# Four-layer image stack on one core: attention sums, one order in the Fourier stage, and all loops written out

## The chip, the cores and the metric

One Trainium2 chip, one of its cores. The metric is the device time of one execution in microseconds; the median of three runs of the kernel before is 20360.88 us (20354.01 to 20361.54).

## The reference, cut to what matters

The input `x` is 2 images of 64 channels, 256 x 256, fp32, held as 128 channels by L = 65536 pixels. Four layers follow one another, each on the group-normalized result of the one before and added to it:

```python
x = x + _L0_conv_ref(_gn(x), img, w_pos, w_img, w_comp)   # attention over 9 shifted neighbours
x = x + _L1_conv_ref(_gn(x), ...)                         # two state-space scans ("mamba") along the pixels
x = x + _L2_conv_ref(_gn(x), w_in, w_dw, fft_filter, w_out) # 8x8 Fourier patches, 3x3 taps, gelu gate
x = x + _L3_conv_ref(_gn(x), q_table, 1)                  # 8x8 cosine transform, rounded

# layer 0
un_em = _unfold3x3(em)                                    # em: 64 maps from image and position
feature_score = jnp.einsum('bckhw,bchw->bkhw', un_em, em)
un_fea = _unfold3x3(inp)
comp_score = jax.nn.sigmoid(jnp.einsum('bckhw,c->bkhw', un_fea, w_comp))
weighted_fea = jnp.einsum('bckhw,bkhw->bchw', un_fea, comp_score * feature_score)
# layer 1, per state n of 16, twice
h = dA_t * h + dBu_t;  y = einsum(h, C_t)
# layer 2
x = einsum(x, w_in); xf = rfft2(patches) * fft_filter; x = irfft2(xf)
x = depthwise 3x3 conv(x); x1, x2 = split(x); x = gelu(x1) * x2; einsum(x, w_out)
```

## The kernel before

Six stages run one after another, each a block in which the five engines have their own instruction streams and meet at semaphores: statistics of x, score maps, attention, mamba, Fourier, cosine transform. Every stream issues in order, so an instruction that waits holds up all that is behind it on its engine.

**Attention** (`attention_layer`, L385 to L680): 64 chunks of 1024 pixels, and a 65th step for the rest. A step has nine neighbours k. TensorE (PE) spreads the score map of k over the channels in PSUM (`p_f`, two banks taken in turns); VectorE (DVE) multiplies it by the shifted input `g` into `apr` k (L657, in the code `pr[k]`); GpSimd (Pool) adds products in pairs (L678): (0,1), (2,3), (4,5), (6,7), and 8 onto 6. PE sums the four results with identity matmuls into `p_a` (`add`, L519 through the helper `halves`): 0, 2, 4 at k = 6, 7, 8 of the step, the last one, 6, at k = 2 of the next. DVE then writes the output (`output`, L632, at k = 4), its statistics (L645, k = 6) and the next `g` (`make_g`, L623, at k = 7). `g` is the input less its mean, times a sigmoid; ScalarE (ACT) reads the score `p_s` from PSUM and writes the sigmoid to SBUF as `sig` (L582), so `make_g` reads two SBUF tiles, `ax` and `sig`.

**Mamba** (`mamba_layer`, L683 to L1377): 64 chunks of 1024, each in four tasks (two layers l, two images b), a task for 16 states n. For 13 of them DVE multiplies (L1305) and then scans (L1311); for three (8, 9, 10) Pool makes the product and DVE only scans. Each scan waits for DVE's own product of the same state (L1307). Pool multiplies every state by C (L1359), PE adds over states (`py`, L1016), ACT makes the decays (L1176). A "turn" is four tasks; turns 2 to 62 of the chunks lie in a loop (L829), 61 times; a turn before it and one behind it, and two tasks at either end, are written out. At the loop's head ACT loads an activation table (L1186). Once in a turn DVE takes the statistics of the output (L1283) and once in a task it gates (L1278).

**Fourier** (`fft_layer`, L1380 to L1992): 64 slots, two for each of 32 stripes of 8 rows. A slot is 24 ticks on PE: `conv` (L1620, taps of unit u), `project` (L1628, L1630: the output product of the slot before, in two parts at ticks 1 and 4), `widen` (L1594: pair p of the next slot, at ticks 1, 3, ... 15), `from_freq` (L1603), and in even slots `turn` and `to_freq` for the next stripe. DVE multiplies what `widen` left in the single PSUM tile `p_fr` by the filter (`filter_`, L1854); it has 30 taps per slot (L1848), the filter of pair p stands ahead of tap 3, 5, 8, ..., and the residual additions (L1870) behind taps 3 and 7.

**Loops.** In every stage a part of the turns is a hardware loop with a counter in a register (L37, L44, L458, L829, L1551, L1684, L1796, L1905, L1974, L2031, L2053); there the semaphore values of waits are computed by register instructions ahead of the wait. Outside of the loops they are constants.

## Time and profile before

| | |
|---|---|
| median of three runs | 20360.88 us |
| the profiled execution | 20351.94 us |
| its span | 20350.2 us |
| attention | about 390 to 1560 us |
| mamba | about 1650 to 16410 us |
| Fourier | about 16523 to 19890 us |
| cosine transform | about 19975 us to the end |
| busy, share of the span: PE, DVE, ACT, Pool | 67%, 90%, 56%, 85% |

The shares are averages over stages that have different limits, so each stage is read for itself. Instructions of registers, branches and semaphores are not counted as busy.

### The profile page before, as it was taken

What the parts mean: (1) busy time and instruction counts of PE and PEld (TensorE: products, weight loads), DVE (VectorE), ACT (ScalarE), POOL (GpSimd) and SP (SyncE); (2) the same over time, 40 slices, a digit from 0 to 9 for tenths busy, and PEclk for the clock granted to TensorE, in tenths of its full rate; (3) what the DMA queues carried; (4) which work ended last, traced back from release to release, by engine and by line L of the source; (5) the groups of instructions that cost most, each with busy time, mean ns of one, the idle gap of its engine ahead of it and who ended that gap; (6) DMA issues with size and microseconds to landing.
All of it is one profiled execution on the core that took longest, in us unless ns stands there. A gap on an engine that the chain in (4) does not pass through costs nothing. (4 is left out here: it accounts for less than half of the span.)

```text
span 20350.2 us, 184019 instructions
## 1 busy us (share of the span) xinstructions
PE 13599.4 (67%) x47074; PEld 4943.0 (24%) x47074; DVE 18393.4 (90%) x11898; ACT 11461.6 (56%) x12716; POOL 17198.0 (85%) x7352
## 2 busy tenths in 40 slices
PE   4885666666666666666666666666666668888885
PEld 2331111111111111111111111111111134444444
DVE  5778999999999999999999999999999978888896
ACT  1115666666666666666566666666666646666663
POOL 3777888888888988888888888888888968888881
PEclk8887777777777777777777777777777789999997
DMA  3224555555545555555555455554555511011113
GB/s 120 94 91 121 134 127 126 129 130 134 128 126 128 131 133 129 126 128 132 131 131 127 127 131 131 131 127 127 130 132 130 128 41 31 25 31 31 31 27 137
DMA packets 615483, 2240.63 MB, mean 110 GB/s; under 512 B 74881, under 2 KB 92147, under 8 KB 591091
## 3 DMA queue, kind: packets, MB, share of 16 engines
q1 hardware_dynamic: 610146, 2232.63, 42.2%
q10 hardware_dynamic: 5265, 7.14, 0.1%
q8 instruction: 33, 0.54, 0.0%
q14 instruction: 39, 0.32, 0.0%
HBM read 990.77 MB, written 174.96 MB: 57 GB/s over the span
## 5 line engine op out<-in xcount | busy, mean ns | idle before, releaser
L1359 POOL TENSOR_TENSOR h<-h,c_bc 128x1024 f32<-128x1024 f32 x4096 | 9620.9, 2359 | 1534.0 <-DVE h L1311 1494.3
L1311 DVE TENSOR_TENSOR_SCAN h<-da,state,px 128x1024 f32<-128x1024 f32 x3328 | 7810.9, 2347 | 559.2 <-PE py L1016 168.6
L1176 ACT ACTIVATE da<-d_bc,a_neg 128x1024 f32<-128x1024 f32 x3328 | 3796.6, 1145 | 3500.2 <-DVE h L1311 3476.0
L1002 PE MATMUL px<-cf,bsel 32*128 32x512 f32 x4096 | 2023.6, 1083 | 3854.4 <-DVE h L1311 3854.4
L1305 DVE TENSOR_TENSOR px<-px,du_bc 128x1024 f32<-128x1024 f32 x3328 | 4099.1, 1232 | 287.8 <-PE px L1002 70.5
L1948 POOL TENSOR_TENSOR acc<-acc,ta 128x1024 f32<-128x1024 f32 (+1 forms) x1040 | 2424.8, 2339 | 492.5 <-DVE acc L1848 366.9
L1016 PE MATMUL py<-h,ysel 128*32 128x512 f32 x16384 | 2393.2, 710 | 96.8 <-POOL h L1359 96.1
L1848 DVE SCALAR_TENSOR_TENSOR p_c<-zb,w_dw,p_c 128x1024 f32<-128x1024 f32 (+1 forms) x1560 | 1987.0, 1274 | 43.7 <-PE p_c L1620 11.2
L1351 POOL TENSOR_TENSOR xs<-du_bc,b_bc 128x1024 f32<-128x1024 f32 x768 | 1807.7, 2354 | 0.0
L1311 DVE TENSOR_TENSOR_SCAN h<-px,state,xs 128x1024 f32<-128x1024 f32 x768 | 1743.1, 2326 | 0.0
L1002 PEld LDWEIGHTS px<-cf,bsel 32*128 32x128 f32 x4096 | 488.7, 290 | 4993.7 <-DVE h L1311 4635.0
L1747 ACT ACTIVATE ta<-zb,w_dw 128x1024 f32<-128x1024 f32 (+1 forms) x1040 | 1168.7, 1128 | 308.7 <-POOL acc L1948 286.9
L1603 PE MATMUL p_i<-basis,v 128*128 128x128 f32 x6144 | 964.4, 294 | 382.9 <-ACT zb L1726 372.8
L1176 ACT ACTIVATE px<-d_bc,a_neg 128x1024 f32<-128x1024 f32 x768 | 855.2, 1114 | 634.1 <-DVE h L1311 630.4
L973 PE MATMUL pm<-hx,w_tap 128*128 128x512 f32 x1024 | 794.0, 946 | 532.8 <-ACT hx L1084 532.8
L678 POOL TENSOR_TENSOR apr<-apr 128x1024 f32<-128x1024 f32 x325 | 824.1, 2543 | 383.4 <-DVE apr L657 377.9
L1620 PE MATMUL p_c<-zb,diag 128*128 128x512 f32 x2064 | 1016.8, 627 | 167.2 <-DVE acc L1848 132.5
L1603 PEld LDWEIGHTS p_i<-basis,v 128*128 128x128 f32 x6144 | 779.6, 193 | 811.1 <-ACT zb L1726 553.7
L1016 PEld LDWEIGHTS py<-h,ysel 128*32 128x32 f32 x16384 | 472.8, 121 | 1891.0 <-issue 1227.0
L657 DVE TENSOR_TENSOR apr<-g,p_f 128x1024 f32<-128x1024 f32 x585 | 690.0, 1214 | 253.5 <-PE p_f L519 252.1
L981 PE MATMUL pm<-hy,w_res 64*128 64x512 f32 x512 | 482.8, 1096 | 620.1 <-ACT u L1094 620.1
L1726 ACT ACTIVATE zb<-p_i 128x384 f32<-128x384 f32 x1024 | 524.4, 512 | 645.9 <-PE p_i L1603 641.7
(222 smaller groups left out, 20126.8 us busy)
## 6 DMA issues: line engine op xcount, KB each, us to landing
d_bc<-delta SPq DMA_DIRECT2D x1024, 512.0 KB, 8.3
du_bc<-du SPq DMA_DIRECT2D x1024, 512.0 KB, 8.2
c_bc<-c_rows_dram SPq DMA_DIRECT2D x1024, 512.0 KB, 4.5
b_bc<-c_rows_dram SPq DMA_DIRECT2D x256, 512.0 KB, 7.9
hx<-x_dram SPq DMA_DIRECT2D x252, 256.5 KB, 5.3
st_x<-in_x_dram SPq DMA_DIRECT2D x32, 1024.0 KB, 4.8
ax<-in_x_dram SPq DMA_DIRECT2D x64, 512.0 KB, 3.4
xr<-x_dram SPq DMA_DIRECT2D x64, 512.0 KB, 5.8
```

What stands on the lines that cost most here:

```text
L1002: last = nc.tensor.matmul(px[(t.par + q + q // 2) % 2][:, cut], bsel[rows, q, :], cf[rows, cut], start=True, stop=True)
L1016: last = nc.tensor.matmul(py[32 * j:32 * j + 32, cut], ysel[:, :], h[:, (4 * q + j) % 8, cut], start=False, stop=(q == Q - 1))
L1176: nc.scalar.activation(out[:, :], d_bc[:, n % J, :], ACT.Exp, scale=a_neg[t.l][:, n:n + 1]).then_inc(da_done, 1)
L1305: nc.vector.tensor_tensor(out=x[:, :], in0=b[:, :], in1=du_bc[:, j, :], op=ALU.mult).then_inc(m1_done, 1)
L1311: nc.vector.tensor_tensor_scan(h[:, n % 8, PAD:T + PAD], a[:, :], x[:, :], state[:, 2 * t.l + t.b, n:n + 1], ALU.mult, ALU.add).then_inc(s ...
L1351: nc.gpsimd.tensor_tensor(out=xs[i][:, :], in0=du_bc[:, n % J, :], in1=b_bc[:, :], op=ALU.mult).then_inc(xs_done, 1)
L1359: nc.gpsimd.tensor_tensor(out=h[:, n % 8, 0:T], in0=h[:, n % 8, PAD:T + PAD], in1=c_bc[q % 2][:, :], op=ALU.mult).then_inc(m2_done, 1)
L1603: last = nc.tensor.matmul(p_i[:, c], v[j // 2 % 2][:, j % 2, c], basis[:, 1, :], start=True, stop=True)
L1620: last = nc.tensor.matmul(p_c[odd(s, u)][:, i * 512:i * 512 + rows * W], diag[:, oc, t, :], zb[b][:, oc, y:y + rows, dx:dx + W], start=(t ...
L1747: nc.scalar.activation(ta[odd(s, u)][t][:, 0:n * W].rearrange("p (y x) -> p y x", y=n), zb[b][:, oc, y:y + n, dx:dx + W], ACT.Identity, sc ...
L1848: nc.vector.scalar_tensor_tensor(out=out, in0=zb[b][:, oc, y:y + n, dx:dx + W], scalar=w_dw[:, oc, m:m + 1], in1=other, op0=ALU.mult, op1= ...
L1948: nc.gpsimd.tensor_tensor(out=acc[h][oc][:, c], in0=acc[h][oc][:, c], in1=ta[o][t][:, c], op=ALU.add).then_inc(added, 1)
```

## The change

Attention: Pool gets a sixth addition, (0,2), after (2,3), and PE adds three results (0 at k = 7, 4 at k = 8, 6 at k = 2 of the next step) instead of four. The sigmoid is written over the score in PSUM; `make_g` reads it there, and the next score waits until `make_g` has read (`g_done`) instead of for the sigmoid. Fourier: in a slot on PE `widen` stands ahead of `project`. All loops are written out: every step, turn and slot is in the program with constant addresses and semaphore values; the table load at the head of the mamba loop is left out.

```diff
-        sig = [sb(f"sig{i}", [128, T]) for i in range(2)]
...
-        PAIRS = [(0, 1), (2, 3), (4, 5), (6, 7), (6, 8)]
-        SUMMED = {0: 1, 2: 2, 4: 3, 6: 5}
+        PAIRS = [(0, 1), (2, 3), (0, 2), (4, 5), (6, 7), (6, 8)]
+        SUMMED = {0: 3, 4: 4, 6: 6}
+        NP, NA = len(PAIRS), len(SUMMED)
...
-                for c in range(3):
-                    step(Step(0, c))
-                with eng.Fori(1, NK // 2 - 1) as m:
-                    for c in (1, 2):
-                        step(Step(m, c))
-                for c in (NK - 1, NK):
-                    step(Step(0, c))
+                for c in range(NK + 1):
+                    step(Step(c))
...
                 if s.from_(1):
-                    pe.wait_ge(sig_done, s.nth(0, 1) - 1)
+                    pe.wait_ge(g_done, s.nth(0, 1) - 1)
                 halves(p_s, comp_s[:, :], x[s.par]).then_inc(s_ps, 1)
...
-                    if k >= 6:
-                        add(s, 2 * (k - 6))
+                    if k == 7:
+                        add(s, 0)
+                    if k == 8:
+                        add(s, 4)
...
-                    if s.from_(2):
-                        act.wait_ge(g_done, s.nth(0, 1) - 2)
-                    nc.scalar.activation(sig[s.par][:, :], p_s[:, :], ACT.Sigmoid, bias=s_bias[:, :]).then_inc(sig_done, 1)
+                    nc.scalar.activation(p_s[:, :], p_s[:, :], ACT.Sigmoid, bias=s_bias[:, :]).then_inc(sig_done, 1)
...
-                                               in1=sig[s.par][:, :], op0=ALU.add, op1=ALU.mult).then_inc(g_done, 1)
+                                               in1=p_s[:, :], op0=ALU.add, op1=ALU.mult).then_inc(g_done, 1)
...
-                    if s.from_(1) and k % 2 == 0 and k < 8:
-                        dve.wait_ge(acc_done, s.nth(k // 2, 4) - 4)
+                    if s.from_(1) and k in SUMMED:
+                        dve.wait_ge(acc_done, s.nth(list(SUMMED).index(k), NA) - NA)
...
-                    if n == 4:
-                        pool.wait_ge(paired, s.nth(3, 5))
+                    if n in (2, NP - 1):
+                        pool.wait_ge(paired, s.nth(n - 1, NP))
...
-            with eng.Fori(2, NK - 1) as k:
-                tasks = turn_tasks(k, k, -2)
...
+        for k in range(1, NK):
+            TASKS += turn_tasks(k)
...
-                if not isinstance(t.turn, int) and t.c == -2:
-                    act.preload_act_table_set("natural_log_exp_and_others")
...
                     if j in CONV_AT:
                         conv(s, b, CONV_AT[j])
+                    if not no_next and j in WIDEN_AT:
+                        widen(ns, r + b, nb, WIDEN_AT[j])
                     if not first and j in PROJECT_AT:
                         project(s - 1, nb, r if rows_left else None, PROJECT_AT.index(j))
                     if not no_next:
-                        if j in WIDEN_AT:
-                            widen(ns, r + b, nb, WIDEN_AT[j])
...
-            with pe.Fori(1, NR - 1) as r:
+            for r in range(1, NR - 1):
```

The other loops (statistics, cosine transform, the other engines of the Fourier stage) are changed like the last one.

## Rows read from the trace of the kernel before

**Rows 1.** Busy time in stretches: us, PE, PEld, DVE, ACT, POOL, PEclk, DMA share, GB/s

```profile
390.00:1560.00 1170.00, 965.66 (x2464) 372.83 (x2462) 906.27 (x846) 139.29 (x128) 824.12 (x325) 0.89 0.28 91
1650.00:16410.00 14760.00, 9397.27 (x28604) 2722.43 (x28604) 13937.42 (x7791) 8945.76 (x9622) 13232.59 (x5683) 0.73 0.51 129
16523.00:19890.00 3367.00, 2752.20 (x13593) 1468.15 (x13591) 3011.12 (x2677) 2118.23 (x2628) 2997.59 (x1274) 0.97 0.11 29
```

**Rows 2.** One line's instructions: the mamba loop's branch on DVE, durations in ns, first and last start

```profile
L829 DVEq COMPARE_BRANCH  x61: 50/56/67, 2187.9 to 16046.1; - x61
```

**Rows 3.** Timeline of DVE: its gates, in written-out tasks before and behind the mamba loop

```profile
1744.60 1.20 DVE L1278 TENSOR_TENSOR yg<-py,sr 128x1024 f32<-128x1024 f32 x1
...
1970.78 1.20 DVE L1278 TENSOR_TENSOR yg<-py,sr 128x1024 f32<-128x1024 f32 x1
...
16059.42 1.20 DVE L1278 TENSOR_TENSOR yg<-py,sr 128x1024 f32<-128x1024 f32 x1
...
16287.41 1.20 DVE L1278 TENSOR_TENSOR yg<-py,sr 128x1024 f32<-128x1024 f32 x1
```

**Rows 4.** Groups by line: statistics in mamba, and the table load; busy us, mean ns

```profile
L1283 DVE BATCH_NORM_STATS2 bn_even<-xo 128x512 f32 (+1 forms) x128 | 80.7, 673 | 16.9 <-POOL xo L1342 16.9
L1186 ACT ACT_TABLE_LOAD x61 | 78.3, 1283 | 1.1
```

**Rows 5.** Waits of DVE, 1963 to 16048 us (mamba loop): us in total, times, longest

```profile
DVE h L1311 <- DVE px L1305: 111.4, 488, 0.3
```

**Rows 6.** Timeline of DVE at a back edge of the mamba loop

```profile
6809.81 1.23 DVE L1305 TENSOR_TENSOR px<-px,du_bc 128x1024 f32<-128x1024 f32 x1
6811.32 2.35 DVE L1311 TENSOR_TENSOR_SCAN h<-da,state,px 128x1024 f32<-128x1024 f32 x1 [0.28 <-DVE px L1305]
```

**Rows 7.** DMA queues in a written-out stretch, 1650 to 1957 us: packets, MB, share

```profile
q8 instruction: 5, 0.08, 0.1%
q14 instruction: 6, 0.05, 0.0%
```

**Rows 8.** DMA queues within the mamba loop, 2187 to 16046 us: the only one listed

```profile
q1 hardware_dynamic: 497314, 1793.55, 51.1%
```

**Rows 9.** Pool's additions in attention: durations min/median/max in ns, first and last start

```profile
L678 POOL TENSOR_TENSOR apr<-apr x325: 2334/2356/3345, 396.2 to 1551.5; 128x1024 f32<-128x1024 f32 x163
```

**Rows 10.** Timeline of Pool over one attention step: start us, us, idle before

```profile
1025.47 2.36 POOL L678 TENSOR_TENSOR apr<-apr 128x1024 f32<-128x1024 f32 x1 [3.12 <-DVE apr L657]
...
1032.37 8.07 POOL L678 TENSOR_TENSOR apr<-apr 128x1024 f32<-128x1024 f32 x3 [1.09 <-DVE apr L657]
1041.95 2.35 POOL L678 TENSOR_TENSOR apr<-apr 128x1024 f32<-128x1024 f32 x1 [1.51 <-DVE apr L657]
```

**Rows 11.** Timeline of DVE over the same step

```profile
1026.44 1.28 DVE L632 SCALAR_TENSOR_TENSOR axo<-p_a,a_gn,axr 128x1024 f32<-128x1024 f32 x1
...
1032.21 1.28 DVE L623 SCALAR_TENSOR_TENSOR g<-ax,mean_n,sig 128x1024 f32<-128x1024 f32 x1
...
1040.65 2.35 DVE L657 TENSOR_TENSOR apr<-g,p_f 128x1024 f32<-128x1024 f32 x2 [2.38 <-PE p_f L519]
```

**Rows 12.** Waits of DVE, 16786 to 19741 us (Fourier)

```profile
DVE v L1854 <- PE p_fr L1594: 278.6, 224, 3.9
```

**Rows 13.** Timeline in an even Fourier slot that began at 16834.9 us

```profile
16838.71 1.98 PE L1628 MATMUL p_qo<-ge,w_out 128*64 128x512 f32 x4
...
16841.67 0.92 PE L1594 MATMUL p_fr<-w_in,ft 64*128 64x384 f32 x4
16842.73 0.96 DVE L1854 TENSOR_TENSOR v<-p_fr,filt 128x768 f32<-128x768 f32 x1 [3.93 <-PE p_fr L1594]
...
16843.74 0.92 PE L1594 MATMUL p_fr<-w_in,ft 64*128 64x384 f32 x4 [1.16 <-DVE v L1854]
```

**Rows 14.** Timeline in the odd slot behind it

```profile
16896.69 0.96 DVE L1854 TENSOR_TENSOR v<-p_fr,filt 128x768 f32<-128x768 f32 x1 [1.27 <-PE p_fr L1594]
...
16897.70 0.92 PE L1594 MATMUL p_fr<-w_in,ft 64*128 64x384 f32 x4 [1.16 <-DVE v L1854]
```

More of the change, by code:

```diff
@@ L36, in _ @@
                 eng.dma_start(xt[i][:, :], src[:, i * T:(i + 1) * T]).then_inc(x_in[i], 16)
-            with eng.Fori(1, NK // 2) as k:
+            for k in range(1, NK // 2):
                 for i in range(2):
@@ L43, in _ @@
         def _(eng):
-            with eng.Fori(0, NK // 2) as k:
+            for k in range(0, NK // 2):
                 for i in range(2):
@@ L549, in step @@
                         score(s.other(1))
[L550 to L553 removed]
+                    if k == 7:
+                        add(s, 0)
+                    if k == 8:
+                        add(s, 4)
+            score(Step(0))
             run(step)(pe)
[L555 removed]
+            add(Step(NK), 6)
         @block.scalar
@@ L664, in step @@
                         make_g(s.other(1))
-            make_g(Step(0, 0))
+            make_g(Step(0))
             run(step)(dve)
-            output(Step(0, NK))
-            statistics(Step(0, NK))
+            output(Step(NK))
+            statistics(Step(NK))
         @block.gpsimd
@@ L877, in spread_b @@
             def spread_b(t):
-                stored = eng.to_reg(16 * t.nth()) if not isinstance(t.turn, int) else 16 * t.nth()
                 if t.from_(1):
                     eng.wait_ge(xs_done, t.nth(NX - 1, NX) - NX)
-                eng.wait_ge(c_out, stored)
+                eng.wait_ge(c_out, 16 * t.nth())
                 first = POOL_X[0] // 4 * 4
@@ L923, in main @@
                 spread_c(t, 1)
-                if t.l == 0 and not (isinstance(t.k, int) and t.k == NK - 1):
+                if t.l == 0 and t.k < NK - 1:
                     load_hx(t)
@@ L1079, in norm_hx @@
                 act.wait_ge(hx_in[b], 32 * t.k + 32)
-                first = isinstance(t.k, int) and t.k == 0
+                first = t.k == 0
                 parts = ((slice(0, 64), slice(2, 3)), (slice(0, 128), slice(3, T + 2))) if first else \
@@ L1144, in back_norm @@
                 act.wait_ge(zn_done, t.nth())
-                later = not isinstance(t.k, int) or t.k >= 1
+                later = t.k >= 1
                 b = t.b
@@ L1550, in _ @@
             at(0)
-            with eng.Fori(1, NR - 2) as r:
+            for r in range(1, NR - 2):
                 at(r)
@@ L1654, in slot @@
                 nb, ns = 1 - b, s + 1
-                rows_left = not (isinstance(r, int) and r == NR - 1)
+                rows_left = r < NR - 1
                 for j in range(TICKS):
@@ L1795, in _ @@
             slot(0, 1, 1)
-            with act.Fori(1, NR - 1) as r:
+            for r in range(1, NR - 1):
                 for b in range(2):
@@ L1843, in tap @@
                 if i == ND - 1:
-                    prev = G(s, h) - 1 if not isinstance(s, int) or s < NS else G(s - 1, 0) + 1
+                    prev = G(s, h) - 1 if s < NS else G(s - 1, 0) + 1
                     ahead(dve, a_done, prev)
@@ L1866, in residual @@
                     ahead(dve, bn_done, r * 2)
-                rows = LOW if isinstance(s, int) and s == 0 else slice(0, 128)
+                rows = LOW if s == 0 else slice(0, 128)
                 c = place_of(s, pos, i)
@@ L1875, in statistics @@
                 n = r * 4 + (2 * pos + i)
-                first = isinstance(r, int) and r == 0 and i == 0
-                if isinstance(s, int) and s == 0:
+                first = r == 0 and i == 0
+                if s == 0:
                     parts = [(LOW, n, W if first else 0)]
@@ L1883, in statistics @@
                 for rows, n, lo in parts:
-                    last = nc.vector.bn_stats(bn3[rows, bass.ds(n, 1), :], xo[rows, at + lo:at + 512])
+                    last = nc.vector.bn_stats(bn3[rows, n:n + 1, :], xo[rows, at + lo:at + 512])
                 if i == 1:
@@ L1904, in _ @@
                 slot(s // 2, s % 2, s)
-            with dve.Fori(2, NR - 1) as r:
+            for r in range(2, NR - 1):
                 for b in range(2):
@@ L1973, in _ @@
             slot(0, 1, 1)
-            with pool.Fori(1, NR) as r:
+            for r in range(1, NR):
                 for b in range(2):
@@ L2030, in run @@
                 step(i, i, 0)
-            with eng.Fori(1, NR // 2) as m:
+            for m in range(1, NR // 2):
                 for i in range(2):
@@ L2041, in step @@
             def step(i, par, m):
-                if not isinstance(i, int) or i >= 2:
+                if i >= 2:
                     eng.wait_ge(y_done, i - 1)
@@ L2052, in _ @@
             step(1, 1, 0)
-            with eng.Fori(1, NR // 2) as m:
+            for m in range(1, NR // 2):
                 for i in range(2):
@@ L2068, in transpose @@
                 k = i * NG + n
-                if not (isinstance(i, int) and k < 2):
+                if k >= 2:
                     pe.wait_ge(t_copied, k - 1)
@@ L2078, in transform @@
                 pe.wait_ge(t_copied, k + 1)
-                if not (isinstance(i, int) and k < 2):
+                if k >= 2:
                     pe.wait_ge(scaled, k - 1)
@@ L2111, in step @@
                     act.wait_ge(t_ps, k + 1)
-                    if not (isinstance(i, int) and k < 2):
+                    if k >= 2:
                         act.wait_ge(d_ps, k - 1)
@@ L2125, in step @@
             def step(i, par, m):
-                if not isinstance(i, int):
+                if i >= 2:
                     dve.wait_ge(y_out[par], m * 16)
```

121 lines of the change are left out of this document (57 added, 64 removed).

## The prediction

> **What bounds the kernel now.** The shares of the whole span name DVE, but the change touches three stages, so the first view is the busy time stretch by stage [rows 1]. In mamba DVE is busy for 13937 of 14760 us; what it idles there, and nothing else, is on offer. In attention nobody is: PE 83%, DVE 77%, Pool 70%, so the stage is bound by a ring of hand-offs, and the second view is a timeline of one step. In the Fourier stage DVE and Pool are both at 89%, and the waits of DVE [rows 12] show that all that it waits for is `p_fr`, the result of `widen`. The reader is to see in each what ends DVE's wait. All three stages follow one another, so what a stage gains, the whole gains.
>
> **Mamba, loop written out.** The length of a turn in the loop is read from the branch: (16046.1 - 2187.9) / 60 = 230.97 us [rows 2]. The trace also holds two turns with constant waits. From gate to gate over four tasks they take 1970.78 - 1744.60 = 226.18 us and 16287.41 - 16059.42 = 227.99 us [rows 3]. The first has no statistics yet; a turn of the loop has, 2 x 0.673 = 1.35 us [rows 4], so it would be 227.5. The gain of a turn is 3.0 to 3.5 us. I take 3.2, since nothing says which end the steady state is nearer to; 61 turns give **-196 us**. Where it lies: in the loop DVE's scan waits for DVE's own product behind a register instruction, 488 times long enough to be listed, 111 us in all [rows 5], and the rest in gaps too short for the list. The back edge itself costs no engine anything: the branch falls into the running scan, and the product behind it starts with no listed idle time at 6809.81 [rows 6]; the wait that follows, 0.28 us, is the register one. The table load, 1.28 us once in a turn on ACT [rows 4], goes; it is hidden under DVE's product of 1.23 us and the wait of 0.28 [rows 6] and is inside of the two measured turns anyway. Outside of the range of both turns I allow 2.5 to 4.0 us a turn, -150 to -244, for a different phase of PE's clock, which stands at 0.73 there [rows 1].
>
> The Trainium skill (Runtime: NRT & Kernel Launch, Instruction fetch mechanics) says that a taken branch whose target isn't at hand forces a fetch and a stall, while straight code streams. By it the back edges would be the loss. The trace doesn't agree for these loops: within the loop no instruction packet is listed at all [rows 8], and DVE runs through the edge.
>
> **Attention.** Take the step from one addition (2,3) on Pool to the next, 1025.47 to 1041.95: 16.48 us [rows 10]. Its ring: Pool can add (6,7) only at 1032.37, when DVE is through output, products 5 to 7 and statistics; then Pool works 8.07 us in a row on (6,7), (6,8) and the next step's (0,1). Three at 2.36 would be 7.08; one of the three took about a microsecond more, 3.34, the maximum of the line [rows 9]. It is the one that `make_g` overlaps from 1032.21 to 1033.49 [rows 11]; the output, which reads one PSUM and one SBUF tile, overlaps the addition of 1025.47 from 1026.44 on and that one took 2.36 [rows 10, 11]. So an operation of DVE with two SBUF inputs holds Pool up, and one with a PSUM input doesn't. With the sigmoid in PSUM `make_g` is of the second kind: (6,7) costs 2.36. The activation's own time and `make_g`'s I leave as they are: output and `make_g` both take 1.28 [rows 11]. After (6,8), at 1032.37 + 3.34 + 2.36 = 1038.07, PE does the last sum and product map 3, and DVE starts product 3 at 1040.65 and ends it at 1041.87, 3.8 us later [rows 11].
>
> The new ring: from the end of product 3 Pool now has (2,3), (0,2), (4,5), (6,7), (6,8), five additions in a row, 5 x 2.36 + 0.1 = 11.9, and 3.8 to the next product 3: 15.7 us. Over DVE's side it would be 1032.37 - 1025.47 = 6.9 to the start of (6,7), 4.7 for two additions and 3.8: 15.4. So Pool becomes the bound, by 0.3, and a step at full clock gains 16.48 - 15.7 = 0.8 us. The PE sum that goes, less than the 2.6 us from (6,8) to product 3, lay in Pool's shadow and gives nothing by itself; sum 0 now waits for (0,2) at k = 7, and behind it on PE stand product map 8, sum 4 and the maps 0 and 1 of the next step, for which DVE waits. (0,2) ends 4.8 us after product 3, product 7 ends at 6.8: the map that waits behind the sum comes at the latest at 4.8 + 2.6 = 7.4, when `make_g` still runs. The score's new wait, for `make_g` of the step before, is met long before. The real mean step is longer: 1155.3 us from the first to the last of 325 additions [rows 9], less some 14 us for the one step that is not whole, over 64 is 17.8, 1.3 above 16.48; PE's clock is 0.89 there [rows 1], and the last sum stands in the ring. I keep the 1.3: 17.0 against 17.8, **-50 us** in 62 steps. Bounds: all of the 1.3 gone as well, -130; the clock rival below, +68.
>
> The Trainium skill (SBUF — State Buffer, Who interferes with whom) agrees on the hold-up: a DVE instruction with two SBUF inputs contends with a GpSimd one that reads SBUF, and with at most one it doesn't. It says further that the loser blocks for the whole instruction; here the addition, which began 0.16 us after `make_g`, lost 0.98 of 1.12 us.
>
> **Fourier.** At tick 1 DVE waits for `widen` of pair 0, which stands on PE behind `project`: 3.93 us in the even slot and 1.27 in the odd one [rows 13, 14]. With `widen` first, it starts in the even slot where `project` did, at 16838.71 [rows 13], where the clock is low (the first half of `project`, four matmuls, took 1.98): 2 x 0.92 = 1.84, and the filter can start at 16840.6, 2.1 earlier. `project` follows, now at the higher clock and so estimated at 2 x 1.98 / 2 = 2.0, and ends at about 16842.6, DVE's filter and its one tap until the residual at 40.6 + 0.96 + 1.28 = 42.8: the residual waits for nothing. But that isn't the slot's gain, since pairs 5 to 7 of even slots wait for PE as well, and PE's chain only moves by the idle time that it loses: 1.16 us before pair 1 in both kinds of slots [rows 13, 14], because DVE filters while PE projects. In the odd slot DVE gains 1.27 and gives 0.2 back two pairs later, where PE comes 1.16 earlier at most. So 1.1 a slot, 62 slots: **-68 us**. Bounds: 0.2 a slot in even ones if `project` stays slow there (31 x 1.3 = -40), 2.1 + 1.27 if nothing holds on (-104). The loops: the same waits of the same size stand in written-out and looped slots; 0, bounded by 0.2 us a slot, -12.
>
> **Statistics and cosine transform**: their waits are for DMAs and PE, 0 to -5 us.
>
> **Sum.** 20351.94 (profiled) - 196 - 50 - 68 = 20038. The median of before stands 9 us higher, so on its footing 20360.88 - 314 = **20047 us**.
>
> **Rivals.** (a) *PE's clock falls.* In attention PE has less to do and waits more. If its clock falls from 0.89 to the 0.73 of mamba [rows 1], the excess grows by 0.27 / 0.11: 1.3 to 3.2, the step is 15.7 + 3.2 = 18.9, +68 instead of -50, in all 20165. For it: one sum of four less; against: the wait before the last sum gets shorter as PE is bound closer to Pool. (b) *The hold-up isn't `make_g`'s inputs.* Then (6,7) stays at 3.34, the ring is 16.7, the step 18.0, +12 us, in all 20109. (c) *The Fourier swap only moves the wait* from filter to residual: nothing there, in all 20115. Against it are the 0.2 us to spare above. (d) *The other side: written-out code arrives late.* In written-out stretches an instruction packet comes every 28 us (5 + 6 in 307 us) [rows 7], in the loop none [rows 8]. Over 14760 + 3367 us that makes some 650 packets. If each one made the stage wait, among the broadcasts that keep the DMA engines 51% busy, 0.48 us would eat all 314; at 0.7 us the kernel would be 20360 - 314 + 455 = 20500. Against it: the two measured turns of mamba ran on such packets and were the faster ones. (e) *Everything adds up better*: 3.5 a turn, 1.3 gone in attention, 1.3 a Fourier slot: 20360.88 - 214 - 130 - 80 = 19937.
>
> **How the numbers follow.** The forecast 0.62; (a) 0.12, (b) 0.07, (c) 0.08, (d) 0.04, (e) 0.07. The range, 19950 to 20170, holds the forecast with its bounds, (b), (c), (a) and an edge of (e). A measurement of this kernel can tell 0.2%, 41 us, from no change; (a) to (c) are all far beyond that. Only (d), or two rivals at once, lead elsewhere: faster 0.94, same 0.02, slower 0.04.
>
> **What would show it.** Mamba: four tasks from gate to gate in 227.5 to 228, and the waits of scan for product gone from the list. Attention: all additions at 2.36, Pool with five in a row, a step of 15.7 at its shortest; DVE waiting for product map 3 only. Fourier: no wait, or one of 1.7 us, ahead of the first filter, and the 1.16 of PE gone; waits at pairs 5 to 7 as before. It would be wrong if DVE idled for "issue" in written-out code (d), if the clock in attention fell below 0.8 (a), or if the residual took over the wait (c).

## The result, and the profile after

| | before | after |
|---|---|---|
| median of four runs | 20361.21 us | 19915.81 us (19912.74 to 19917.03) |
| ratio, 95% interval | | 0.9781 [0.9765, 0.9798] |
| profiled execution, its span | 20351.94, 20350.2 us | 19915.19, 19913.4 us |

The kernel became 445 us faster. The forecast was 314, and the time lies under the range, whose low end was 19950. Stage by stage, the spans of the two profiled executions are as follows; each runs from the end of the one before to its own last result, and attention begins at the end of its first `make_g`.

| stage | before | after | difference | forecast |
|---|---|---|---|---|
| up to attention | 393.8 | 390.1 | -3.7 | 0 to -5, with the cosine transform |
| attention | 1164.2 | 1070.1 | -94.1 | -50 |
| mamba | 14857.6 | 14623.1 | -234.5 | -196 |
| Fourier | 3536.5 | 3440.1 | -96.4 | -68 |
| cosine transform | 398.0 | 389.9 | -8.1 | with the first |

The five differences make -437. The other 9 us of the 445 are that the profiled execution of before was itself 9 us under its median.

Busy time by stage, the view of [rows 1], for attention, mamba and Fourier of the kernel after (columns as there):

```profile
390.00:1465.00 1075.00, 829.13 (x2198) 305.04 (x2198) 909.51 (x852) 136.50 (x127) 913.55 (x390) 0.93 0.31 100
1560.00:16183.00 14623.00, 9398.76 (x28804) 2742.84 (x28803) 13963.29 (x7818) 8851.19 (x9581) 13224.84 (x5681) 0.73 0.52 131
16300.00:19523.00 3223.00, 2630.81 (x13206) 1418.72 (x13204) 2932.76 (x2634) 2064.32 (x2566) 2940.89 (x1263) 0.97 0.12 31
```

In mamba the busy time of DVE is what it was; what went is idle time. In attention the granted clock rose from 0.89 to 0.93, and both Pool and DVE are now at 85%.

**Mamba.** The waits of DVE in the former loop's stretch, and its timeline around three scans (start, duration, idle before):

```profile
DVE h L1299 <- PE py L1006: 147.8, 192, 1.2
DVE px L1293 <- PE px L992: 84.0, 122, 0.7
DVE h L1299 <- DVE px L1293: 6.3, 35, 0.5
...
2249.44 1.23 DVE L1293 TENSOR_TENSOR px<-px,du_bc 128x1024 f32<-128x1024 f32 x1
2250.71 2.35 DVE L1299 TENSOR_TENSOR_SCAN h<-da,state,px 128x1024 f32<-128x1024 f32 x1
```

The 488 waits of a scan for DVE's own product [rows 5] are 35. A scan starts 0.04 us behind the end of its product (2250.67 to 2250.71), where in [rows 6] it was 0.28, the longest of the kinds there; the usual one in the loop of before was 0.12. A turn takes 227.13 us instead of 230.97 [rows 2].

**Attention.** Pool's additions (minimum, median, maximum of the durations in ns), and Pool's timeline:

```profile
L673 POOL TENSOR_TENSOR apr<-apr x390: 2339/2357/2377, 392.5 to 1453.7; 128x1024 f32<-128x1024 f32 x195
...
1013.27 2.36 POOL L673 TENSOR_TENSOR apr<-apr 128x1024 f32<-128x1024 f32 x1 [1.21 <-DVE apr L652]
1016.22 9.48 POOL L673 TENSOR_TENSOR apr<-apr 128x1024 f32<-128x1024 f32 x4 [0.59 <-DVE apr L652]
1026.15 2.36 POOL L673 TENSOR_TENSOR apr<-apr 128x1024 f32<-128x1024 f32 x1 [0.45 <-DVE apr L652]
1030.03 2.36 POOL L673 TENSOR_TENSOR apr<-apr 128x1024 f32<-128x1024 f32 x1 [1.52 <-DVE apr L652]
1032.97 12.00 POOL L673 TENSOR_TENSOR apr<-apr 128x1024 f32<-128x1024 f32 x5 [0.59 <-DVE apr L652]
```

No addition takes 3.34 us any more [rows 9]. Four or five stand in a row: 9.48 is 4 x 2.357 and 0.05, 12.00 is 5 x 2.357 and 0.21. The step is read from one output to the next: 1017.19, 1033.94, 1049.74, 1065.55 are 16.75, 15.80 and 15.81 us. The mean over the stage is 16.39, before 17.88.

**Fourier.** An even slot, in which the filter of before waited for 3.93 us [rows 13]:

```profile
16496.57 1.99 PE L1608 MATMUL p_c<-zb,diag 128*128 128x512 f32 x4 [3.35 <-DVE acc L1836]
...
16498.48 0.92 PE L1582 MATMUL p_fr<-w_in,ft 64*128 64x384 f32 x4
16499.33 1.08 PE L1616 MATMUL p_qo<-ge,w_out 128*64 128x512 f32 x4
16500.27 0.95 DVE L1842 TENSOR_TENSOR v<-p_fr,filt 128x768 f32<-128x768 f32 x1
...
16502.33 0.68 DVE L1858 TENSOR_TENSOR fxo<-p_qo,fxr 128x512 f32<-128x512 f32 x1
...
16507.16 3.60 PE L1608 MATMUL p_c<-zb,diag 128*128 128x512 f32 x8
...
16511.66 0.96 DVE L1842 TENSOR_TENSOR v<-p_fr,filt 128x768 f32<-128x768 f32 x1 [1.56 <-PE p_fr L1582]
```

`widen` (16498.48) stands ahead of `project` (16499.33), the first filter and the residual (16502.33) wait for nothing, and the next wait is that of the filter of pair 2, 1.56 us, behind two convolutions in a row. Over the stage DVE waits 202.4 us for `p_fr`, at the most 1.6 us; that is 3.3 us in each of 62 slots, where it was 278.6 in 56, 5.0 us each [rows 12]. Two slots take 102.4 us, before 105.6.

### The profile page after: what moved, and what is told of

Same layout as the page of the kernel before. It is cut to its first block and busy times, and to the rows that moved or that the text cites. A ratio compares the mean times of both kernels' runs of the same rounds, so it can differ in the third digit from the quotient of the medians.

```text
span 19913.4 us, 150486 instructions
## 1 busy us (share of the span) xinstructions
PE 13363.6 (67%) x46814; PEld 4859.7 (24%) x46814; DVE 18395.2 (92%) x11898; ACT 11358.4 (57%) x12655; POOL 17285.6 (87%) x7417
## 5 line engine op out<-in xcount | busy, mean ns | idle before, releaser
L673 POOL TENSOR_TENSOR apr<-apr 128x1024 f32<-128x1024 f32 x390 | 913.5, 2356 | 198.2 <-DVE apr L652 185.1
```

## The experiments

Three questions: which part moved which stage, what in a written-out mamba made the turn shorter, and what the loops' back edges cost. Every time is a median; a run with one execution has no interval. "Before" and "after" are the two kernels; a diff is against the one that is named.

### The edits with the loops kept

Before, with the sixth addition, the sigmoid in PSUM and `widen` in front, as in the change; all loops stay.

> The kernel before with all three edits (sixth addition, sigmoid in PSUM, widening first), loops kept. Theory E (the edits alone make what attention and the Fourier stage gained): the attention step stays at 16.4 us as in the changed kernel (17.88 before), the Fourier stage gains its 97 us, mamba stays at 230.96 us a turn; total about 20361 - 92 - 97 = 20172. Rival W (writing out the loops gave the part beyond the forecast, 45 us in attention and 29 in Fourier): the step is 17.0 to 17.1, the Fourier stage gains 68; total about 20245.

Measured: 20525.41 us, 1.0082 [1.0065, 1.0099], slower than before. Attention 1053.3 us (step 16.12), two Fourier slots 102.43 us: both gains are there without a single loop written out. What ate them is mamba, in which nothing was edited: 237.02 us a turn, (16300.5 - 2079.4) / 60 from the branch's first and last start. The loop's branch in this kernel, DVE's timeline behind one back edge, DVE's waits in the loop, and the DMA queues in the loop:

```profile
L829 DVEq COMPARE_BRANCH  x61: 55/63/63, 2079.4 to 16300.5; - x61
...
2318.24 2.35 DVE L1311 TENSOR_TENSOR_SCAN h<-da,state,px 128x1024 f32<-128x1024 f32 x1
2324.71 1.23 DVE L1305 TENSOR_TENSOR px<-px,du_bc 128x1024 f32<-128x1024 f32 x1 [4.13 <-issue]
2328.18 2.35 DVE L1311 TENSOR_TENSOR_SCAN h<-da,state,px 128x1024 f32<-128x1024 f32 x1 [2.24 <-issue]
...
DVE h L1311 <- issue: 166.9, 48, 5.9
DVE px L1305 <- issue: 161.4, 58, 6.2
...
q1 hardware_dynamic: 484453, 1747.12, 49.9%
q14 instruction: 291, 2.38, 0.1%
```

In before nothing of this kind is listed: the branch falls into the running scan [rows 6] and no instruction packet moves in the loop [rows 8]. Here 291 move in 58.5 turns, 5 at each back edge, and DVE stands still for "issue" twice behind it ("issue" is idle time for which the profile shows nothing that was waited for), 6.4 us at this edge. The turn is 6.05 us longer, and the mamba stage 362 us. The mamba code of the two kernels is the same; what differs ahead of it is the length of the instruction streams (on DVE five instructions fewer, counted in the two traces with each loop's body once). Whether placement is the cause is tried further down; here it is only seen that the same loop can run without fetches or pay for them at every edge.

### The loops alone

After, with the attention edits and the Fourier order taken back:

```diff
-        PAIRS = [(0, 1), (2, 3), (0, 2), (4, 5), (6, 7), (6, 8)]
+        PAIRS = [(0, 1), (2, 3), (4, 5), (6, 7), (6, 8)]
...
-                    nc.scalar.activation(p_s[:, :], p_s[:, :], ACT.Sigmoid, bias=s_bias[:, :]).then_inc(sig_done, 1)
...
+                    nc.scalar.activation(sig[s.par][:, :], p_s[:, :], ACT.Sigmoid, bias=s_bias[:, :]).then_inc(sig_done, 1)
...
-                    if not no_next and j in WIDEN_AT:
-                        widen(ns, r + b, nb, WIDEN_AT[j])
                     if not first and j in PROJECT_AT:
...
+                        if j in WIDEN_AT:
+                            widen(ns, r + b, nb, WIDEN_AT[j])
```

> All loops written out, attention and the order in the Fourier stage as before. Theory E: mamba 227.1 us a turn, attention step 17.8, Fourier unchanged, cosine transform 8 us shorter; total about 20361 - 234 - 12 = 20115. Rival W: attention and Fourier give 45 and 29 us more, total about 20041.

Measured: 20132.01 us, 0.9887 [0.987, 0.9903]: -229 us. Mamba has 227.15 us a turn, all of its gain; Fourier's two slots take 105.8 us (before 105.6), so there writing out gives nothing and the whole gain is the swap's; the cosine transform takes 389.8 us, all of its gain. Attention's step became longer, 18.14 against 17.88.

### One engine's mamba stream at a time

First, in before: only DVE's stream of the mamba loop is written out, PE, ACT, Pool and SP keep the loop (and, for attention, the sixth addition alone). Second, the mirror image: all but DVE written out (and the sigmoid alone).

```diff
-            with eng.Fori(2, NK - 1) as k:
+            if eng.engine in WRITTEN_OUT:
+                for k in range(2, NK - 1):
+                    at = 4 * k - 2
+                    tasks = turn_tasks(0, k, at)
+                    run(tasks, Task(0, at - 1, 1, 1, k - 2), Task(0, at + 4, 0, 0, k + 1), {1: k - 2})
+            else:
+              with eng.Fori(2, NK - 1) as k:
                 tasks = turn_tasks(k, k, -2)
...
+        WRITTEN_OUT = (mybir.EngineType.DVE,)
```

> Mamba: only VectorE's stream is written out, the other engines keep their loops and the table load. Attention: loops kept, only the sixth addition, sigmoid still in SBUF. Fourier as before. Theory R (VectorE's own register waits between product and scan make the turn long): 227.1 to 227.6 us a turn, gaps of the scan behind its product fall from 6.3 to 1.8 us a turn. Rival O (the other engines' register waits or the table load): it stays at 230 to 231. Attention: if the hold-up by the two SBUF inputs stays, the ring at full clock is 16.7 to 16.8 and the mean step 17.0 to 18.0; if the sixth addition alone were enough, 16.4.

> Mamba: all engines written out but VectorE, which keeps its loop. Attention: loops kept, only the sigmoid in PSUM, five additions. Fourier as before. Theory R: 230 to 231 us a turn. Rival O: 227 to 228. Attention: Pool's additions all at 2.36 us; the ring loses the hold-up of 0.98 us, 16.48 to 15.5 at full clock; if PE's clock stays as it was the mean step is 16.9, if the fourth sum is what cools PE it stays above 17.

Measured: 227.35 us a turn with DVE alone written out, 230.95 with all others written out and DVE in the loop. The waits of DVE in mamba, first of the one and then of the other:

```profile
DVE h L1322 <- PE py L1027: 161.0, 209, 1.2
DVE h L1322 <- DVE px L1316: 4.8, 28, 0.2
```

```profile
DVE h L1316 <- PE py L1021: 160.0, 241, 0.8
DVE h L1316 <- DVE px L1310: 110.3, 484, 0.3
```

So the turn's gain hangs on DVE's own stream; the other engines' streams are worth about 0.2 us of the 3.84. A turn has 52 pairs of product and scan; in four of them (three or four in after) the scan waits for `py`. In the others, summed over all gaps, short ones too, DVE stands between product and scan for 6.32 us a turn in before and 1.84 in after. The usual gap is 0.123 us in before (35 a turn; 8 are 0.28, and 5 are 0.036) and 0.036 in after. Of these 4.5 us 0.5 come back between scan and next product (2.73 to 3.27) and 0.3 in the wait for `px` (1.07 to 1.38), 0.2 are won at `py`. The turn gains 3.84.

For attention the same two runs give the parts: the sixth addition alone 17.06 us a step, the sigmoid alone 16.26, both 16.12 (loops kept), neither 17.88. They don't add.

### The sigmoid in SBUF again

After, with the sigmoid written to `sig` and read from there by `make_g`; the sixth addition stays.

> The changed kernel with the sigmoid back in SBUF, all else kept. If the hold-up of Pool lies in make_g's two SBUF inputs, 65 additions take 3.34 us again and the ring of five additions is 15.8 + 1.0 = 16.8 us at full clock; mean step 17.1 to 17.5 against 16.39 (with loops the sixth addition alone gave 17.06). Rival (the hold-up does not lie there): 16.4. Mamba 227.1 us a turn and Fourier as in the changed kernel.

Measured: 19960.06 us, step 17.05. The groups of Pool's additions in attention, of this kernel, and of after (busy us, mean ns | idle before):

```profile
L676 POOL TENSOR_TENSOR apr<-apr 128x1024 f32<-128x1024 f32 x328 | 821.4, 2521 | 111.6 <-DVE apr L655 96.0
```

```profile
L673 POOL TENSOR_TENSOR apr<-apr 128x1024 f32<-128x1024 f32 x342 | 801.2, 2357 | 130.9 <-DVE apr L652 119.2
```

The mean of an addition is 0.164 us longer, six times that 0.98 a step: one addition a step with the microsecond that the prediction saw in [rows 9]. In all kernels with the sigmoid in PSUM, with five additions or six, none takes over 2.39. This settles that `make_g`'s second SBUF input is what holds Pool up.

It holds DVE up as well. With six additions `make_g` starts while an addition still has 0.43 us to run; `make_g` itself (minimum, median, maximum in ns), of this kernel and of after:

```profile
L621 DVE SCALAR_TENSOR_TENSOR g<-ax,mean_n,sig x64: 1278/1516/2118, 388.6 to 1458.7; 128x1024 f32<-128x1024 f32 x64
```

```profile
L618 DVE SCALAR_TENSOR_TENSOR g<-ax,mean_n,p_s x64: 1272/1274/1280, 388.8 to 1415.5; 128x1024 f32<-128x1024 f32 x64
```

With two SBUF inputs it takes 0.24 us longer than with the sigmoid in PSUM, and the addition that starts behind it 0.98. The section of the Trainium skill that the prediction names (SBUF — State Buffer, Who interferes with whom) agrees. What the same page of the Trainium skill states (SBUF — State Buffer, SBUF: two separate sides), that the one that starts second blocks for the whole instruction of the other, fits the order in both cases, but the time lost is less than the time shared: 0.98 of 1.12 us, and 0.24 of 0.43. What makes the difference is not shown.

### Five additions with the sigmoid in PSUM

After, without the sixth addition (four sums on PE again).

> The changed kernel without the sixth addition: five on Pool, four sums on PE, the sigmoid in PSUM. With loops the sixth addition brought 0.14 us a step beyond the sigmoid (16.26 to 16.12). Written out, Pool's addition that waits for Pool's own last one starts 0.143 us behind it instead of 0.078, and the sixth addition has one such wait more. Theory P (that wait costs what it measures): 16.26 + 0.1 to 0.2 = 16.4 to 16.5, the same as the changed kernel within 0.1 us a step, 19910 to 19925 in all. Rival C (the fourth sum keeps PE colder in written-out code): 16.7 or more, 19935 and up.

Measured: 19905.98 us (19904.36 to 19909.47), 0.9775 [0.9759, 0.9792], step 16.22. It is 10 us faster than after, and no run of one lies among those of the other, though the intervals of the ratios overlap. The steps come in two lengths in these two kernels, by whether PE's clock falls to the lower level in them: 15.6 and 17.3 us here, 15.8 and 16.8 in after. So the sixth addition lengthens the short step, as the prediction's ring says, which it binds to Pool, and it shortens the long one; written out the two together are a loss of 0.17 us a step, with the loops kept (above: 16.26 and 16.12) they were a gain of 0.14. Beside the sigmoid it is no part of the gain.

### The last sum later, and `widen` first at every tick

The timeline of after shows where a step of 16.8 us loses its microsecond: the first sum, four matmuls at PE's lower level (1.2 of 2.4 GHz), is on the ring, and the map of product 8 behind it is late.

```profile
1004.38 3.14 PE L514 MATMUL p_a<-apr,a_mats 128*128 128x512 f32 x4 [0.88 <-POOL apr L673]
1007.31 1.06 PE L514 MATMUL p_f<-fb,fsel 96*128 96x512 bf16 x2
1008.41 1.22 DVE L652 TENSOR_TENSOR apr<-g,p_f 128x1024 f32<-128x1024 f32 x1 [0.93 <-PE p_f L514]
1009.71 2.35 POOL L673 TENSOR_TENSOR apr<-apr 128x1024 f32<-128x1024 f32 x1 [0.76 <-DVE apr L652]
```

At the higher level the same sum takes 1.88 to 1.99. The edits, in after:

```diff
-                    if k == 2 and s.from_(1):
+                    if k == 3 and s.from_(1):
                         add(s.other(-1), 6)
...
-                    if j in CONV_AT:
-                        conv(s, b, CONV_AT[j])
                     if not no_next and j in WIDEN_AT:
                         widen(ns, r + b, nb, WIDEN_AT[j])
+                    if j in CONV_AT:
+                        conv(s, b, CONV_AT[j])
```

> The changed kernel with the last sum of a step at k = 3 of the next instead of k = 2, and with the widening ahead of the convolution at every tick of the Fourier slot. Attention: if the ring runs through sum and map 3, taking map 3 out of it leaves Pool's own 6 x 2.36 = 14.2 and DVE's 14.5 plus hand-offs: 15.2 to 15.6 a step, 50 to 70 us less. If instead the clock rules, 16.4 as before. Fourier: the wait of 1.56 us ahead of pair 2 in even slots stands behind a convolution of 3.6 us; with the widening first it goes, and 0.6 to 1.5 us per even slot with it, 20 to 45 us in all; the rival is that DVE then waits for the convolution instead, 0 or a loss.

Measured: 19822.79 us, 0.9735 [0.9719, 0.9751]. Attention 1004.1 us (step 15.36, either 14.4 to 14.7 or 16.4), Fourier 3406.3 us (two slots 101.6). Pool now works up to seven additions without a wait:

```profile
1015.32 16.80 POOL L673 TENSOR_TENSOR apr<-apr 128x1024 f32<-128x1024 f32 x7 [1.09 <-DVE apr L652]
```

This beats both kernels, the one after by 93 us: 66 in attention and 34 in the Fourier stage, less 7 in mamba, where nothing was edited. Product 3 no longer waits behind a sum that waits for Pool's last addition, so the 3.8 us from (6,8) to product 3, which the prediction took as fixed, leave the ring.

### The loop's head moved, in before

Before, with 23 one-column memsets on DVE ahead of the mamba loop.

> The kernel before, with 23 one-column memsets ahead of the mamba loop on VectorE and nothing else: that moves the loop's first instruction by the same 23 places by which the three edits had moved it when the loops were kept. Theory F (the place of the loop's head among the fetched blocks decides whether the back edge fetches): about 237 us a turn instead of 230.96, a gap of 4.4 us behind the branch, some 290 instruction packets within the loop; total about 20361 + 365 = 20726. Rival (the attention edits change something in mamba's data or timing): 231, 20362.

Measured: 20363.35 us, 0.9999 [0.999, 1.0009], 230.96 us a turn, no fetch in the loop. The expected fetches did not come. The number 23 was wrong: the edits had made DVE's stream ahead of the loop five instructions shorter, not 23 longer. So this run tells only that not every shift hurts.

### The loop's head moved, in the kernel with its loops kept

The kernel of the first experiment, with 16 memsets of that kind ahead of the mamba loop and nothing else changed:

```diff
             nc.vector.memset(state[:, :, :], 0.0)
+            for i in range(16):
+                nc.vector.memset(shift[:, i:i + 1], 0.0)
```

> The kernel with the three edits and the loops kept, plus 16 one-column memsets on VectorE ahead of the mamba loop. The 23 memsets of the run before were too many to repeat the shift: counted in the traces, the edits had moved the loop's head by about 5 places forward, not by 23 backward. Theory F (place of the loop among the fetched blocks): 16 places back takes the head between two places that didn't fetch, so the turn is 231 us again, no instruction packet in the loop, and the total 20525 - 365 = 20160. Rival (the edits themselves disturb mamba): 237 us a turn, 20526.

Measured: 20146.61 us, 0.9894 [0.9878, 0.9911]: 16 instructions more make the kernel 379 us faster. 230.97 us a turn; the queues within the loop:

```profile
q1 hardware_dynamic: 497314, 1793.61, 51.3%
q8 instruction: 2, 0.03, 0.0%
q14 instruction: 1, 0.01, 0.0%
```

The 291 packets of q14 have become one. So the place of the loop in DVE's stream decides whether a back edge fetches: beside the 16 instructions and the small tile that they write nothing differs. Which places do, the runs don't tell: of four that were seen (before, before shifted, this one and the first experiment) one does.

This run also splits the change: with the loops in a good place the edits bring 215 us (20361 to 20147) and writing out 231 more (20147 to 19916); writing out alone brought 229.

### The waits written as registers, without loops

After; DVE's wait for its own product and Pool's for its own last addition compare with a register, filled by a move right ahead, instead of with a constant:

```diff
-                        dve.wait_ge(m1_done, t.nth(TILED.index(n), NM))
+                        dve.wait_ge(m1_done, dve.to_reg(t.nth(TILED.index(n), NM)))
...
-                        pool.wait_ge(paired, s.nth(n - 1, NP))
+                        pool.wait_ge(paired, pool.to_reg(s.nth(n - 1, NP)))
```

> The changed kernel, all written out, with two kinds of waits against a register instead of a constant: in mamba VectorE's scan for VectorE's own product (13 a task), in attention Pool's addition for Pool's own last one (2 a step). Theory R (the register wait between product and scan is what the loop cost): the gap of the scan behind its product goes from 1.8 to 5 or more us a turn and the turn from 227.1 to 230 or more. Rival (it is the number of register instructions of all kinds on VectorE's stream): below 229. Attention, theory S (a Pool instruction that waits for a constant of its own engine starts 0.065 us later than one whose wait stands in a register instruction): the hand-off falls from 0.143 to 0.078 and the step from 16.39 to 16.1 to 16.3, as with loops; rival: no change.

Measured: 19905.59 us, 227.24 us a turn, product to scan 1.84 us a turn as in after: a register in the wait costs DVE nothing as such. What differs is which instruction holds the wait. A scan waits for two things, DVE's own product and ACT's decay, and one of the two waits stands in an instruction of the sequencer ahead of the scan. In after and here that is the decay's (L1295), which is done while the product runs, and the scan itself holds the wait for the product. In the loop of before it is mostly the product's (a register instruction, L1307). But for five scans a turn it is the other way round there too, and these start as soon as those of after. Both kinds stand side by side in the loop of before:

```profile
6798.68 1.23 DVE L1305 TENSOR_TENSOR px<-px,du_bc 128x1024 f32<-128x1024 f32 x1
6799.95 2.35 DVE L1311 TENSOR_TENSOR_SCAN h<-da,state,px 128x1024 f32<-128x1024 f32 x1
6802.33 1.23 DVE L1305 TENSOR_TENSOR px<-px,du_bc 128x1024 f32<-128x1024 f32 x1
6803.69 2.35 DVE L1311 TENSOR_TENSOR_SCAN h<-da,state,px 128x1024 f32<-128x1024 f32 x1
```

The first scan holds the wait for its product and starts 0.036 us behind it; ahead of the second the register instruction holds it, and the gap is 0.123. The 0.28 of [rows 6] has two more sequencer instructions behind that one. The 0.5 us that came back in after are of the same kind: five products a turn that held their wait for the last scan in before (0.034 us) have it in an instruction ahead in after (0.10 or 0.13). So the form is what costs the time.

On Pool the form counts in the same way, though it was the register here that made it the better one. In after a wait instruction (L672) ahead of the addition holds the wait for Pool's own last addition, and the next one starts 0.143 us behind that last addition. Here, and in the loops, the instruction ahead (a MOVE here, a register instruction there) holds the wait for DVE's product, the addition itself holds the one for Pool's own, and the gap is 0.078:

```profile
1023.78 11.86 POOL L673 TENSOR_TENSOR apr<-apr 128x1024 f32<-128x1024 f32 x5 [1.10 <-DVE apr L652]
```

Five in a row in 11.86 us here, 12.00 in after (above). The attention step fell from 16.39 to 16.14, what it was in the kernel with its loops kept (16.12). A step at the higher level went from 15.80 to 15.67, which is the two waits; the rest of the 0.25 is that 34 of 63 steps lie wholly at that level, where in after it is 25, and why is not shown. In the kernel with only the loops written out (18.14 against 17.88 above, 17 us in all) there is one such wait a step, 0.07 of the 0.27; the rest is again in the steps with a low clock.

### Five additions with the later sum

> As the run with the later sum and the widening ahead of every convolution (19823), but with five additions on Pool and four sums on PE. The attention step was 15.36 with six. If Pool's six additions still bound it (14.2 of 15.4), five free it and the step falls to 15.0 or less, 20 to 30 us in all; if PE is what it waits for there, or its clock, the fourth sum makes it longer: 15.5 to 16, 10 to 40 us more.

Measured: 19831.93 us, 0.974 [0.9724, 0.9757], step 15.41. The sixth addition is worth 9 us here, with ranges that don't overlap (19831.66 to 19834.10 and 19819.05 to 19827.01), though the intervals of the ratios do. Once Pool's last addition is off the ring, the sum that the sixth addition saves PE seems to count a little; by the intervals it is not certain.

### The later sum, and Pool's waits as registers

> e7_later_sum_widen_first with one more edit: Pool's waits for its own last addition compare with a register (written in the MOVE ahead) instead of a constant. In e10_register_waits the same edit, made in the changed kernel, took the attention step from 16.39 to 16.14. Theory S (Pool's own hand-off is on the ring, and its form sets 0.143 or 0.078 us): two hand-offs a step stand in e7 too, where Pool is bound closer; the step goes from 15.36 to 15.1 to 15.25, 7 to 16 us in 62 steps, median 19807 to 19816. Rival: with the last sum a product later the ring no longer runs through the hand-off (0,2) or (6,8) but through PE's cold stretch; the step stays at 15.36 and the median at 19823, both within 5 us. Mamba (227.2 a turn) and Fourier (101.6 for two slots) stay by both.

Measured: 19819.87 us (19810.26 to 19823.06), 0.9733 [0.9717, 0.975]. The step is 15.27, 0.09 less, between the two expectations; attention is 4.6 us shorter, and the median 3 us, within the rival's 5 us and not to be told from nothing. The hand-offs themselves did shrink, to six additions in 14.19 us, 0.04 over 6 x 2.357:

```profile
999.00 14.19 POOL L673 TENSOR_TENSOR apr<-apr 128x1024 f32<-128x1024 f32 x6 [1.09 <-DVE apr L652]
```

So with the sum moved only part of the ring runs through them. It is the fastest kernel of the study, by less than can be measured.

## Why the prediction was off

The direction, the stages and what was to go in each held; the sizes were all too small, and on one side. Of the 131 us that were missed, mamba has 39, attention 44, Fourier 28, the first stage and the cosine transform 12, and 9 are the offset between the profiled execution of before and its median.

**Mamba: 3.2 us a turn, measured 3.84.** The mechanism stands (the register wait of scan for product), and so does "the back edge costs nothing" for the loop as it lay in before. (61 turns of 3.2 are 195 us, not 196.) The step that failed is that the two written-out turns of before bound the steady state to 3.0 to 3.5. They are no steady turns: the last one, 227.99 us [rows 3], takes 227.95 in the kernel after as well, 0.8 above the mean of the turns between. Its own gaps showed the term better. In the trace of before, the gaps between DVE's product and its scan sum to 6.32 us in a looped turn and to 1.71 in that written-out one, 4.6 us; the listed waits [rows 5] are 111 / 61 = 1.8 us a turn of it, and the rest lay under the list's threshold, where the prediction mentioned it without counting. In after it is 1.84, and 0.6 of the 4.5 us came back as other gaps. The bound of 4.0 held.

**Attention: 17.0 us a step, measured 16.39.** The ring at full clock was forecast at 15.7, and a step at full clock takes 15.80. The step that failed is "I keep the 1.3": the excess of the mean step over the one at full clock is 0.6. It isn't that fewer steps have a low clock (39 of 63 in before, 38 in after) but that such a step costs less: it takes 16.8 us, 1.0 over one at full clock, where in before it was 18.7, 2.2 over. The clock rose, where rival (a) had it fall; the bound of -130 had room for it. It did not need the sum that PE no longer makes. The view of [rows 1] in 473 to 1370 us, of before and of the kernel with the sigmoid alone (four sums, loop kept):

```profile
473.00:1370.00 897.00, 745.71 (x1909) 289.47 (x1908) 700.18 (x654) 108.82 (x100) 636.74 (x252) 0.90 0.29 94
473.00:1370.00 897.00, 771.57 (x2109) 298.37 (x2108) 772.81 (x722) 119.27 (x111) 655.09 (x279) 0.96 0.32 104
```

With the sigmoid moved and all four sums kept the clock went from 0.90 to 0.96, with PE busier; with the sixth addition alone it is 0.93. Why it rises with either is not shown. Of the two edits the sigmoid was priced rightly: with it alone the step at full clock is 15.5, and the prediction's sum over DVE's side gives 15.4. The sixth addition, for which the prediction built a new ring with Pool at five in a row, gives nothing beside it. Writing out, put at nothing in attention, cost 17 us.

**Fourier: 1.1 us a slot, measured 1.6.** The wait of 3.93 is gone, not cut to 1.8, and no wait of 3.9 is left in the stage. The size of 1.1 was not too small in itself; the clock was left out of it. Two slots without a stretch at the lower level and two with one, in before and then in after:

```profile
18642.20:18745.30 103.10, 84.46 (x432) 45.88 (x432) 94.38 (x84) 64.99 (x82) 92.49 (x40) 1.00 0.11 31
17160.20:17266.00 105.80, 87.15 (x432) 46.48 (x432) 94.37 (x84) 66.74 (x83) 94.16 (x41) 0.97 0.11 30
```

```profile
16807.50:16909.40 101.90, 83.87 (x434) 45.88 (x432) 94.26 (x85) 66.80 (x84) 94.20 (x41) 1.00 0.12 32
16909.40:17013.10 103.70, 85.56 (x432) 46.46 (x432) 94.34 (x85) 68.50 (x86) 95.93 (x41) 0.97 0.12 31
```

At like clock a slot became 0.6 us shorter (103.1 to 101.9 for two) or 1.1 (105.8 to 103.7). The rest is that the longer kind became rarer: of 28 pairs of slots in the middle of the stage 23 were of it in before and 8 in after, and PE was at the lower level for 167 of 2956 us, and then for 69 of 2866. The step that failed is that the clock was taken to change nowhere but in `project`. By an estimate from these figures some 0.7 of the 1.6 us is that. Why the stretches became rarer is not shown; the kernel with its loops kept has 103 us of them and the same 102.4 us for two slots, so their sum alone does not set the time. "The loops: 0" was right (105.8 with the loops alone written out).

**Statistics and cosine transform: 0 to -5, measured -12.** Nothing was worked out there, and no run looked for the cause beyond that it is the writing out.

**The rivals.** (a) to (c) are out: the clock rose; additions fell to 2.36 with the sigmoid moved and with nothing else; the swap brought the Fourier stage's gain by itself (94 us with the loops kept). (d), late code, did not come in straight code, with 800 instruction packets in the span (q8 377, q14 423) and no wait for "issue" among DVE's in mamba; the longest of the rest, 3.4 us at the head of the Fourier stage, is in before too. But fetches can cost, in loops. The prediction cited the Trainium skill's rule (Runtime: NRT & Kernel Launch, Instruction fetch mechanics) that a taken branch whose target isn't at hand stalls, and set it aside, since [rows 8] show none. That was right for the loop of before and would have been wrong as a general reading: [rows 8] show one placement, and in another, of four, the stall comes, 6.05 us at each edge. With its loops kept, the same change would have been 0.8% slower than before, a case of 20525 us that the prediction didn't have. (e), everything adds up better, was nearest, with 19937 against 19916, in part by luck: its terms -214, -130 and -80 were measured as -234, -94 and -96.

**The range.** Its low end, 19950, cut off (e), of which the prediction says that it holds an edge, although three terms had open ends on that side: the bounds named for mamba, attention and Fourier (-244, -130, -104) sum to 19883. Each estimate had been taken from the careful side (give-backs, a kept excess), and so they missed together.

## What to carry to other kernels

Sum all gaps behind one kind of instruction, also those too short for the list of waits, before pricing what a cheaper wait is worth, and compare a looped and a written-out turn by the gaps behind one instruction rather than by their lengths. Look at which instruction holds the wait for an engine's own last result: it is cheapest in the instruction that waits, and a change of a constant into a register, or of a loop into straight code, can move it either way. A hardware loop that runs without fetches may start to fetch at every back edge after an edit in another stage: look at the instruction packets within the loop, and at "issue" behind the branch, in every build. When an engine is freed, move what stands in front of the operand that the bound engine waits for; that gave more (93 us) than the addition that was put in.

## What the runs showed of the hardware

- A back edge of this loop costs nothing or 6 us (5 packets of 8 KB, DVE idle for 4.13 and 2.24 us behind it), by where the loop lies: 16 instructions of DVE ahead of it made the kernel 379 us faster.
- A wait of an engine for its own last instruction is cheapest in the waiting instruction itself: 0.036 us on DVE and 0.078 on Pool. In an instruction of the sequencer ahead it is 0.10 (a wait instruction) or 0.12 (a register instruction) on DVE and 0.143 (a wait instruction) on Pool.
- A DVE instruction of 1.28 us with two SBUF inputs adds 0.98 us to an addition of Pool that starts just behind it (mean 2521 against 2357 ns, one in six); with one input in PSUM it adds nothing that shows (maximum 2377). The other way, such an instruction that starts 0.43 us before the end of an addition takes 1.52 us instead of 1.28.
